# A two-layer graph network: the edge attribute scores move from the finish of layer 0 into the edge stage of layer 1

## The reference, cut to what matters

```python
xp = (x @ W).reshape(n, HEADS, C)
a_src = jnp.einsum('nhc,hc->nh', xp, att_src)
a_dst = jnp.einsum('nhc,hc->nh', xp, att_dst)
ep = (edge_attr @ W_e).reshape(-1, HEADS, C)
a_edge = jnp.einsum('ehc,hc->eh', ep, att_edge)
alpha = jax.nn.leaky_relu(a_src[src] + a_dst[dst] + a_edge, NEG_SLOPE)
...   # softmax over the edges of each destination
msg = xp[src] * attn[:, :, None]
out = jax.ops.segment_sum(msg, dst, num_segments=n)
```

## Time and profile before

| | us |
|---|---|
| median of 3 runs | 7169.67 |
| the runs | 7134.72, 7169.67, 7181.61 |
| span of the profiled execution | 6304.8 |
| the median above that span | 864.9 |
| layer 0 finish in the span | about 2202 to 2580 |
| layer 1 edge stage in the span | about 3939 to 5137 |

### The profile page before, as it was taken

One profiled execution on the slowest core, in us unless ns is written; L12 is line 12 of the kernel. 1 busy time (PEld: TensorE's weight loads), 2 busy tenths in 40 slices (PEclk: granted clock), 3 DMA queues, 4 the chain that ended last, 5 costly groups with the idle time before them and its releaser, 6 DMA issues. The chain is left out here.

```text
span 6304.8 us, 86879 instructions
## 1 busy us (share of the span) xinstructions
PE 4738.7 (75%) x21453; PEld 3441.8 (55%) x21454; DVE 3946.3 (63%) x9373; ACT 2615.3 (41%) x5007; POOL 3177.3 (50%) x3260
## 2 busy tenths in 40 slices
PE   6966677877778798499899346465566659999999
PEld 4753355656656588366566335344444436666665
DVE  6864379999999877322222677677777764444443
ACT  1531055555555433144444211666666632222222
POOL 2777367777777477277777100777777720000000
PEclk9988888888888855599999557677777779999999
DMA  2004588888888696343443128766666640000000
GB/s 57 1 1 124 173 255 249 249 252 246 250 249 249 201 219 161 108 99 97 106 98 93 27 65 272 208 178 177 177 177 177 178 138 18 14 11 13 14 18 12
DMA packets 616359, 852.78 MB, mean 135 GB/s; under 512 B 209716, under 2 KB 419611, under 8 KB 615645
## 3 DMA queue, kind: packets, MB, share of 16 engines
q0 software_dynamic: 159136, 383.90, 22.7%
q1 hardware_dynamic: 319069, 416.74, 20.9%
q10 hardware_dynamic: 137972, 50.36, 3.3%
HBM read 692.76 MB, written 164.70 MB: 136 GB/s over the span
## 5 line engine op out<-in xcount | busy, mean ns | idle before, releaser
L1340 POOL DMA_INDIRECT b_got<-tmp_l_table,b_src x928 | 982.8, 1059 | 405.7 <-issue 268.0
L2444 POOL DMA_INDIRECT w_got<-tmp_l_table,w_src x928 | 880.5, 949 | 284.5 <-issue 273.9
L3158 POOL DMA_INDIRECT t_got<-tmp_f_table,t_src x672 | 634.3, 944 | 240.7 <-issue 202.0
L1586 PE MATMUL b_pk<-b_keys,b_hot_t 128*128 x1856 | 567.0, 459 | 226.8 <-issue 154.5
L2693 PE MATMUL w_pa<-w_got,w_hot 128*128 128x264 f32 x1856 | 593.3, 474 | 99.3 <-DVE w_got L2600 97.1
L1586 PEld LDWEIGHTS b_pk<-b_keys,b_hot_t 128*128 128x128 f32 x1856 | 398.7, 226 | 317.9 <-issue 255.6
L3617 DVE SCALAR_TENSOR_TENSOR l_accs<-l_po,l_prob,l_accs 128x256 f32 (+1 forms) x392 | 173.5, 480 | 597.6 <-PE l_po L3723 597.6
L2693 PEld LDWEIGHTS w_pa<-w_got,w_hot 128*128 128x128 f32 x1856 | 409.5, 232 | 205.5 <-issue 122.7
L3668 ACT ACTIVATE l_h<-l_ph,l_bn 128x896 f32<-128x896 f32 x224 | 245.0, 1096 | 661.2 <-PE l_ph L3713 661.2
L1601 PE MATMUL b_pa<-b_got,b_hot 128*128 128x260 f32 x1856 | 492.7, 413 | 6.2 <-DVE b_acc L1513 2.2
L1601 PEld LDWEIGHTS b_pa<-b_got,b_hot 128*128 128x128 f32 x1856 | 389.2, 212 | 85.7 <-issue 14.8
(11 more groups left out here) (570 smaller groups left out, 10213.8 us busy)
## 6 DMA issues: line engine op xcount, KB each, us to landing
tmp_g_acc<-b_acc SPq DMA_DIRECT2D x232, 260.0 KB, 3.8
w_spread<-tmp_g_rel_rows SPq DMA_DIRECT2D x232, 256.0 KB, 3.8
t_spread<-tmp_f_rel_rows SPq DMA_DIRECT2D x170, 256.0 KB
b_spread<-tmp_g_rel_rows SPq DMA_DIRECT2D x116, 256.0 KB, 5.8
e_attr<-in_edge_attr ACTq DMA_DIRECT2D x103, 256.0 KB, 4.1
tmp_f_experts<-t_y SPq DMA_DIRECT2D x28, 896.0 KB, 4.7
yl_y<-tmp_f_experts SPq DMA_DIRECT2D x28, 896.0 KB, 10.9
b_got<-tmp_l_table,b_src POOLq DMA_INDIRECT x928, 4.3
```

What stands on the lines that cost most here:

```text
L1340: pool.indirect_dma_start(out=got[:, m % NB, u, :], out_offset=None, in_=T["l0_table"], in_offset=bass.IndirectOffsetOnAxis(ap=src[:, m * ...
L1586: mm = pe.matmul(pk[:, b % 2, u * D:(u + 1) * D], hot_t[:, (at * B4 + b) % HB, u * P:(u + 1) * P], keys[:, bass.ds(tile[u // 2], 1), :], s ...
L2444: pool.indirect_dma_start(out=got[:, p % 3, u, :], out_offset=None, in_=T["l1_table"], in_offset=bass.IndirectOffsetOnAxis(ap=src[:, p * R ...
L3158: pool.indirect_dma_start(out=got[:, g % DEPTH, u, :], out_offset=None, in_=T["f_table"], in_offset=bass.IndirectOffsetOnAxis(ap=src[:, g ...
```

## The change

The 104 blocks leave the finish. In the layer 1 edge stage each round p from 0 to 49 handles two of them, 2(p+2) and 2(p+2)+1, two rounds ahead of their use; four come ahead of round 0. `edge` now stays in SBUF of that stage, so its store, its load and the scratch tensor in memory are gone. The loads are issued by SP, behind the four `spread_rel` transfers of a round, and wait until the block that last used their buffer is turned. There are three load buffers instead of eight, one buffer for the turned block instead of four, and one PSUM bank for turned block and scores together: block n is turned only when block n-1 is kept. VectorE waits in every round until its blocks are kept. In the finish ScalarE has only `gates` and `n.scalar` left, and TensorE nothing until the projection.

```diff
-    RING = 8
-    BANKS = 4
-    PER = 16
+    RING = 3
+    AHEAD = 2
...
-        self.p_turn = s.ps("p_turn", [P, self.BANKS, 512])
-        self.p_edge = s.ps("p_edge", [P, self.BANKS, 512])
+        self.p_turn = s.ps("p_turn", [P, 512])
+        self.p_edge = self.p_turn[:, 0:self.TILES * H]
...
-    def load(self, act, T, n, slot):
+    def load(self, sp, T, n, slot):
         rows, to = T["edge_attr_64"], self.attr[:, slot, :, :]
+        if not isinstance(n, int) or n >= self.RING:
+            sp.wait_ge(self.turned, n - self.RING + 1)
...
+    def turn(self, pe, K, n, slot, turn):
+        pe.wait_ge(self.attr_in[slot], 16 * (turn + 1))
+        if not isinstance(n, int) or n:
+            pe.wait_ge(self.edge_ready, n)
...
# finish, sync
-            edges.store(sp, T, 0, 6 * E.PER)
...
# finish, scalar
-            with act.Fori(1, CHUNKS - 2) as c:
-                chunk(c, E.PER, E.RING)
...
+            with act.Fori(0, CHUNKS) as c:
+                gates(c)
+                n.scalar(act, K, c)
...
# layer 1 edge stage, sync
-            sp.dma_start(edge[:, :, :], T[L.name + "_edge"]).then_inc(edge_in, 16)
+            edges.params(sp, T)
+            for n in range(2):
+                edges.load(sp, T, n, n)
...
+                for k in range(1, 4):
+                    spread_rel(3 * i + k)
+                    load_attr(3 * i + k, k)
...
# scalar, in round_
                 hot_of(-1, 2)
+                if kept is not None:
+                    edges.keep(act, kept)
                 hot_t_of(2)
...
                 apart_of(1)
+                if scored:
+                    edges.copy(act, first)
                 hot_t_of(3)
                 hot_of(-1, 3)
                 apart_of(2)
+                if scored:
+                    edges.keep(act, first)
...
                 hot_of(0, 0)
+                if scored:
+                    edges.copy(act, first + 1)
                 apart_of(3)
...
# vector, in score
+                dve.wait_ge(edges.edge_ready, min(2 * p + 2, SCORED) if isinstance(p, int) else 2 * p + 2)
...
# tensor, in round_
                 hop_of(0)
                 sums_of(0)
+                if not isinstance(p, int) or 2 <= first <= SCORED:
+                    edges.score(pe, first - 1)
                 expand_of(0)
                 hop_of(1)
                 sums_of(1)
                 expand_of(1)
+                if scored:
+                    turn_attr(0)
                 hop_of(2)
                 sums_of(2)
                 expand_of(2)
+                if scored:
+                    edges.score(pe, first)
                 expand_of(3)
                 sums_of(3)
+                if scored:
+                    turn_attr(1)
                 hop_of(3)
```

More of the change, by code:

```diff
@@ L1930, in params, with vector @@
         sp.dma_start(self.att[:, :], bcast_rows(T["L1_gnn_att_edge"].rearrange("h c -> (h c)"), P)).then_inc(self.we_in, 16)
[L1932 to L1937, removed]
+    def vector(self, dve, link):
         A, H = self.A, self.H
@@ L1967, in keep @@
-    def keep(self, act, n, m):
+        sp.dma_start(to[0:odd, whole, :], rows[at + whole * P:self.L.edges, :]).then_inc(self.odd_in, 16)
+        sp.wait_ge(self.odd_in, 16)
+        sp.dma_start(to[:, 0:whole, :], rows[at:at + whole * P, :].rearrange("(u p) a -> p u a", p=P)).then_inc(self.attr_in[slot], 16)
+    def turn(self, pe, K, n, slot, turn):
+        pe.wait_ge(self.attr_in[slot], 16 * (turn + 1))
+        if not isinstance(n, int) or n:
+            pe.wait_ge(self.edge_ready, n)
+        for k in range(self.TILES // 2):
+            mm = pe.transpose(self.p_turn[:, k * P:(k + 1) * P],
+                              self.attr[:, slot, 2 * k:2 * k + 2, :].rearrange("p u a -> p (u a)"), K["ident"][:, :])
+        mm.then_inc(self.turned, 1)
@@ new lines, in copy, with score @@
+    def copy(self, act, n):
+        act.wait_ge(self.turned, n + 1)
+        act.activation(self.attr_t[:, :, :], self.p_turn[:, :].rearrange("p (a e) -> p a e", e=P), ACT.Copy).then_inc(self.attr_t_ready, 1)
+    def score(self, pe, n):
+        pe.wait_ge(self.attr_t_ready, n + 1)
+        w = 2 * self.H
+        for k in range(self.TILES // 2):
+            mm = pe.matmul(self.p_edge[:, k * w:(k + 1) * w], self.attr_t[:, k, :], self.ve[:, :], start=True, stop=True)
+        mm.then_inc(self.edge_out, 1)
@@ L2474, in round_ @@
             def round_(p, k, ahead, now_, behind):
+                first = 2 * (p + edges.AHEAD)
+                kept = first - 1 if not isinstance(p, int) or 2 <= first <= SCORED else None
+                scored = not isinstance(p, int) or first < SCORED
                 def hot_of(q, b):
@@ L2510, in _ @@
             act.wait_ge(set_up, 2)
+            for n in range(2):
+                edges.copy(act, n)
+                if n == 0:
+                    edges.keep(act, n)
             round_(-1, 2, True, False, False)
@@ L2665, in _ @@
                     round_(3 * i + 3 + k, k, i + 1, True, True, True)
-            link.leave(17)
-            for p in range(54, ROUNDS):
+            link.leave(16)
+            for p in range(51, ROUNDS):
                 round_(p, p % 3, p // 3, True, True, True)
@@ L2714, in hop, with round_, turn_attr @@
                     pe.transpose(p_weight, exps[:, :], K["ident"][:, :]).then_inc(weights_out, 1)
-            def round_(p, k, ahead, now_, behind):
+            def round_(p, k, ahead, now_, behind, turn=0):
+                first, at = 2 * (p + edges.AHEAD), 2 * (k + edges.AHEAD)
+                scored = not isinstance(p, int) or first < SCORED
+                def turn_attr(a):
+                    edges.turn(pe, K, first + a, (at + a) % edges.RING, 2 * turn + (at + a) // edges.RING)
                 if ahead:
```

120 lines of the change are left out of this document (36 added, 84 removed).

## The result

The changed kernel takes 7221.57 us (median of 4 runs, 7197.24 to 7228.37) against 7170.01 us (7134.72 to 7181.61), a ratio of 1.0079 [1.0049, 1.0109]. It is slower by 0.8%; 7124 us and a gain were forecast.

A forecast was written before the change was run, and what follows sets the result against it. The finish was taken as a VectorE chain lengthened by ScalarE's two answers, the edge stage as paced by GpSimd's gathers. Waits of 30.7 and 13.1 us and 2.1 us at the start go: -45.9 + 0, 7124 us, range 7085 to 7215.

The forecast's parts named there:

- the base of the sum: Whole kernel: profiled span 6304.8 us plus 864.9 us lying around it gives the median of 7169.7 us.
- GpSimd sets the pace: Layer 1 edge stage: the 16 gathers of a round take 20.05 us, and the other engines wait for or behind them.
- the term of 0 for the edge stage: Edge stage: two added blocks make a round at most 19.9 us, below the gathers' 20.05, so no loss.
- slack of 10.5 us: Edge stage: the sums freeing a gather buffer end 10.5 us early; other engines can lag that much before GpSimd stops.
- cover of 4.0 us a round: Edge stage: VectorE waits 4.0 us a round for gathered rows, so without gathers a round takes about 16.1 us.
- its own test: Edge stage: the forecast is wrong if the stage from 3939 to 5137 grows by over 15 us.
- the round gets longer than the gathers: Rival, edge stage: blocks stand in the chain, a round costs 20.05 to 22.6 us, total 7124 to 7241; chance 0.18.
- TensorE's 3.8 us a round: Edge stage: TensorE's cost of two blocks a round, at the stage's mix of half and full clock.
- I cost it at no change: Projection behind the finish, on TensorE: it started after a long TensorE pause before and does so now; 0 us.
- The clock: Rival, edge stage: thin block work keeps TensorE's clock down, 26.5 us a round, 312 us lost, 7436; chance 0.09.
- Transfers: Edge stage: block loads raise the DMA share, taken as no change; rival that gathers slow, 88 us, 7212, chance 0.05.
- The rival of a projection at full clock: Projection: it gets the full clock because blocks no longer precede it, 30 us more gain, 7094; chance 0.05.

The follow-up runs named there:

- small_spread: Kernel before with only the finish changed, no blocks in the edge stage, 24 one-column matmuls a round at the blocks' four places: 0.9925 of before, faster chip, 20.08 us a round.
- kept_busy: Changed kernel plus 72 unread transposes of a constant on TensorE in each of the finish's seven chunks: 1.0094 of before on a slower chip, projection 137.3 us.
- loads_alone: Changed kernel with only the loads of the blocks in the edge stage, no TensorE or ScalarE work on them: 0.9982 of before, 24.97 us a round.
- tensor_alone: Changed kernel with the blocks' TensorE work and loads, without ScalarE's copies and keeps or the engines' waits on blocks: 1.0251 of before, 28.55 us a round.
- behind_hops_2: Changed kernel with the blocks' turns, scores, copy and keep moved out of the round's own chain, on a slower chip: 1.0279 of before, 28.36 us a round.

## Why the prediction was wrong

**The step that failed is the base of the sum**: "The sum is made against the profiled execution: span 6304.8 us and, for what lies around it, 864.9 us". That put 865 us outside the stages. They lie in them: on a chip like that of the runs, a round of the edge stage takes 24.1 us and not 20.05. Nothing in the rows said that time around a span can be 12% of it; it was taken over without a reason.

**"GpSimd sets the pace"** and the term of 0 for the edge stage rested on that. On the slower chips GpSimd waits for sums (158.5 us), so there is no slack of 10.5 us and no cover of 4.0 us a round. The stage lost 78.5 us in the two profiles, of which 14.9 before the first weighed row, which the prediction had no term for, 68.5 in rounds 1 to 49 and 2.8 in the round before them; what follows gave 7.7 back.

**On the faster chip the edge stage still failed its own test** (over 15 us): 19.8 us. The failing sentence is "Without gathers a round would therefore take about 20.05 - 4.0 = 16.1 us". The 4.0 us of the earlier trace rows are not free: the jump of VectorE's loop lies in them. Where VectorE waits for no gather at all (before, slower chip), it is still idle for (4.6 + 2 x 0.96) / 3 = 2.2 us a round at this place, so only about 1.8 of the 4.0 us were cover, and the jump grew with the change. The rival "the round gets longer than the gathers" is what happened there, at 0.4 us a round. How much of it is TensorE's 3.8 us a round and how much the jump, no run separates.

**The finish, by terms, faster chip**: chunks -42.5 us, where -43.8 was forecast (30.7 + 13.1); start -7.7 for -2.1 (the block loads, named as 0 to 5 us more and set to 0, are the likely rest); projection -6.1 for 0. The projection goes with its clock and not with the change: 87.6 us at 0.61, 93.7 at 0.56 before, and with the changed finish again about 96 at 0.52 in small_spread. That small_spread's 47 us is so near the forecast's 45.9 is in part luck: its chunks and start gain 50 us, more than was forecast, and its projection takes 2 back. VectorE's wait for the gate is gone from the profile, and that for the standard deviation is 2.6 us in seven waits, as forecast:

```profile
DVE e_rstd L975 <- ACT e_sd L983: 2.6, 7, 0.4
```

**The finish, slower chips**: chunks -69.5 in this pair and -46 and -51 by the two other profiles of the old finish, more than forecast. In this pair's profile of the kernel before, VectorE waited 73 us for the gate and the deviation, against 46 in the earlier trace rows; late signals of TensorE ahead of ScalarE's two answers would explain it. But projection +41.9 (+35 to +48 by all profiles). Its first group of matmuls, of the kernel before and then of the changed one, both on a slower chip:

```profile
2904.47 5.99 PE L2265 MATMUL e_p_turn<-h_w,h_xt 128*128 128x16 f32 x28
...
2910.50 0.28 DVE L2179 COPY h_row<-e_p_turn 128x112 f32<-128x112 f32 x1 [8.24 <-PE e_p_turn L2265]
```

```profile
2837.77 11.97 PE L2219 MATMUL h_pt<-h_w,h_xt 128*128 128x16 f32 x56
...
2852.39 0.28 DVE L2163 COPY h_row<-h_pt 128x112 f32<-128x112 f32 x1 [17.71 <-remote]
```

Before, `h_row` starts as the first 28 matmuls end; after, it starts 14.6 us after the first of them began, for the same work. "I cost it at no change" was wrong there. All twelve profiles without blocks in the finish, on slower chips, have 134.8 to 137.3 us, with TensorE at rest before or (in two of them) busy for a third of the time. The three with blocks have about 90 to 100. Why the blocks kept the holds away from the projection stays open.

**The clock** did not go down: 0.76 in both windows above, and on the faster chip 0.80 where the earlier trace rows had 0.77:

```profile
4500.00:5000.00 500.00, 359.55 (x1902) 287.11 (x1902) 365.35 (x1089) 351.45 (x832) 370.50 (x392) 0.80 0.74 196
```

That rival is out for the changed kernel. By the Trainium skill (TensorE: Matmul & The Clock Gate, Part 1: "activity releases the throttle") the clock should have risen. The traces agree only weakly: with 12% more of the time busy it rose by 0.03 in this window on the faster chip (0.01 over the whole stage), and not at all on a slower one. In the finish the blocks kept it busy for 40 us of 40 at 0.50, while kept_busy's bursts of transposes, 69 us of 200, were granted 0.66:

```profile
2600.00:2800.00 200.00, 68.93 (x488) 67.50 (x489) 192.75 (x280) 20.88 (x27) 164.55 (x123) 0.66 0.33 98
```

**Transfers**: a gather is 948 ns before and after, so that rival is out as it was put. What loads_alone leaves open is said above. The rival of a projection at full clock did not come either: its clock is 0.56 before and after on a slower chip.

**What stays open**: what holds TensorE on four chips of five. Shown is that the engines that wait for its matmuls go on 2 to 12 us after the recorded end (medians of 6 to 8 us in seven profiles), in 1.2 to 1.5 places a round without blocks and 1.8 to 2.3 with two whole blocks a round (the faster chip has none), that in tensor_alone its instructions also stop with operands ready, that this does not happen on the fifth chip with the same programs, and that neither a loop written out nor a partly busy engine changes it. VectorE's and GpSimd's own instructions take as long on both kinds of chip (a weighing 1.25 us, a gather 948 ns), so it is not that everything runs slower. Not shown is why the changed stage has more late signals and loses 1 to 1.5 us a round. That the new waits let one hold stop three engines is what one timeline shows, and since tensor_alone loses more without them, they are not the whole cause. tensor_alone and behind_hops_2 show that other orders of such work cost up to 4.4 us, and none of my placements cost less.

## What to carry to other kernels

Before costing anything, compare the profiled span with the run times: a gap like the 12% here can mean that the trace is of another execution than the one that is measured, and it must be found, not carried along as a constant. An engine's wait "for a transfer" can hold a jump of that engine, so it is not slack to its full length: look at the rounds with and without the jump apart. A wait added between two engines is priced by how late its signal can come; behind_hops_2 shows what it costs to leave no other work between a signal and the wait for it, while no run here shows a placement that gains. And measure one program twice: here that alone gave 0.3%.

## What was not expected of the hardware

The same program took 6306 us on one chip and 7087 to 7151 us on four others, with the same 948 ns a gather and with the last stage equal (1166 to 1171 us in all profiles; there TensorE is busy nearly throughout). The difference sits in the stages in which TensorE exchanges signals with the others: 20.06 against 24.10 us a round. VectorE's jump back in its loop, with 3 rounds in the body, left it idle for 4.0 to 9.7 us (other rounds from 0.95), with up to 2.8 us more inside the next group, and 8 KB packets of the queue `q14 instruction` came in that time. TensorE was granted a clock of 0.66 while it ran bursts of transposes for a third of the time, and 0.50 while the blocks kept it busy all the time.
